# Expert weights split during the attention steps, routing in two halves, first steps reordered

## The reference

```
a   = (LN(x) Wq^T)(LN(x) Wk^T)^T * D^-0.5 + adj      12 heads of 32
x   = x + softmax(a) (LN(x) Wv^T + bv) Wo^T + bo      a row of zeros gives 0
u   = LN(x);  logits = mean over nodes(u) router_w^T + router_b
e0, e1 = the two greatest of 4 experts; gates = softmax of their logits
y   = sum over k of gate_k * (act_ek(u w1[ek] + b1) w2[ek] + b2) + u
out = x + LN(y) * ln_g + ln_b                         act: gelu, silu, mish, gelu
```

## Time and profile before

| | us |
|---|---|
| median of three runs | 1681.1 |
| the profiled execution, its own time | 1679.88 |
| its span in the profile | 1678.1 |
| PE busy | 1598.1 (95%) |
| DVE busy | 1191.3 (71%) |
| ACT busy | 953.4 (57%) |
| POOL busy | 826.9 (49%) |
| DMA moved | 159.32 MB, mean 95 GB/s |

### The profile page before, as it was taken

The page is one execution under the profiler, slowest core; times in us unless marked ns, Lnnn a source line. Parts: engine busy times, 40 slices in busy tenths (PEclk is TensorE's granted clock), DMA queues, the critical chain, the costliest instruction groups (busy, mean ns, idle before and its releaser), DMA issues.

```text
span 1678.1 us, 44889 instructions
## 1 busy us (share of the span) xinstructions
PE 1598.1 (95%) x12732; PEld 1531.1 (91%) x12733; DVE 1191.3 (71%) x3613; ACT 953.4 (57%) x2780; POOL 826.9 (49%) x1239
## 2 busy tenths in 40 slices
PE   6999999999999999837999999999999999999997
PEld 6899999999999999727999999999999999999997
DVE  4788888888888887776666665666776766567764
ACT  4888888888888888744332332332433423243332
POOL 2777777777777777760233333323333233323333
PEclk9999999999999999958999999999999999999999
DMA  7233333333333332550122222222222222221221
GB/s 242 67 116 114 120 121 121 116 116 121 121 121 121 121 119 97 178 216 20 62 72 70 70 70 70 70 70 70 70 70 70 70 70 70 70 70 62 79 64 36
DMA packets 81260, 159.32 MB, mean 95 GB/s; under 512 B 8672, under 2 KB 46560, under 8 KB 80992
## 3 DMA queue, kind: packets, MB, share of 16 engines
q1 hardware_dynamic: 81120, 157.58, 27.6%
HBM read 94.64 MB, written 62.91 MB: 94 GB/s over the span
## 4 chain that ended last, share of the span: by engine, by line
PE 88%; DVE 5%; ACT 2%; issue 2%; SPq 1%; POOL 1%; DMA 1%; DVEq 0%; POOLq 0%; ACTq 0%
PE bank L368 68%; PE bank L437 5%; PE bank L526 5%; PE bank L396 3%; PE bank L460 3%; PE bank L477 2%; PE bank L469 1%; PE bank L446 1%; DMA x_in<-in_x 1%; DVE half_t L1027 1%; DVE inverse L1034 1%; DVE inverse L1030 1%; ACT at_hi L688 1%; ACT inverse L721 1%; ACT prob L599 1%
## 5 line engine op out<-in xcount | busy, mean ns | idle before, releaser
L368 PE MATMUL bank<-w_hi,ut_in 128*128 x1536 | 423.2, 343 | 32.3 <-issue 27.9
L599 ACT ACTIVATE prob<-att,neg_max 128x128 f32<-128x128 f32 x768 | 297.4, 391 | 34.4 <-DVE neg_max L871 34.3
L368 PEld LDWEIGHTS bank<-w_hi,ut_in 128*128 128x128 f32 x1536 | 280.8, 189 | 37.0 <-issue 37.0
L987 DVE SCALAR_TENSOR_TENSOR at_lo<-bank,gate_col,at_hi 128x384 fp32r<-128x384 f32 x256 | 146.1, 613 | 185.2 <-ACT at_hi L688 185.2
L368 PE MATMUL bank<-w_hi,at_hi 128*128 x768 | 258.0, 336 | 5.6 <-DVE at_lo L987 5.6
L368 PE MATMUL bank<-w_lo,ut_in 128*128 x768 | 257.9, 336 | 0.0
L368 PE MATMUL bank<-w_hi,at_lo 128*128 x768 | 257.1, 335 | 0.0
L368 PE MATMUL bank<-w_lo,at_hi 128*128 x768 | 256.7, 334 | 0.0
L688 ACT ACTIVATE at_hi<-bank,gate_col 128x384 fp32r<-128x384 f32 x256 | 134.5, 576 | 202.9 <-PE bank L526 201.0
L845 POOL TENSOR_SCALAR rs_z<-mv_z 128x1 f32<-128x1 f32 x64 | 14.7, 229 | 473.8 <-DVE mv_z L1053 473.8
L712 ACT ACTIVATE hid<-hid 128x384 f32<-128x384 f32 x192 | 95.1, 527 | 268.9 <-DVE hid L999 268.9
(11 more groups left out here) (136 smaller groups left out, 3820.9 us busy)
## 6 DMA issues: line engine op xcount, KB each, us to landing
xu_scratch<-xu SPq DMA_DIRECT2D x64, 384.0 KB, 2.3
ut_scratch<-ut_out SPq DMA_DIRECT2D x64, 384.0 KB, 2.7
ut_in<-ut_scratch SPq DMA_DIRECT2D x64, 384.0 KB, 2.9
xz<-xu_scratch SPq DMA_DIRECT2D x64, 384.0 KB, 3.0
x_in<-in_x SPq DMA_DIRECT2D x32, 384.0 KB, 4.4
xu<-in_x SPq DMA_DIRECT2D x32, 384.0 KB, 3.5
out_dram<-xz SPq DMA_DIRECT2D x64, 192.0 KB, 1.9
w_lo<-in_L_ffn_w SPq DMA_DIRECT2D x8, 1152.0 KB, 9.8
```

Of the source, the lines that this page charges most:

```text
L368: last = nc.tensor.matmul(acc, lhs[c][a], rhs[c][b], start=start and n == 0, stop=stop and n == len(terms) - 1)
L599: nc.scalar.activation(prob[g][:, hh, :], att[g][:, head, :], ACT.Exp, bias=neg_max[g][:, head:head + 1], scale=-1.0, accum_out=row_sum[g] ...
L987: nc.vector.scalar_tensor_tensor(out=flat(at_lo[:, s * DC:(s + 1) * DC, :]), in0=at_ps[s][:, 0:HALF], scalar=gate_col[:, col, 1:2], in1=fl ...
```

## The change

Each expert weight is cut into six pieces of 128x384: `PIECES` = 24 pieces of w1 and 24 of w2. From step 5 to step 52 each attention step splits one piece (ACT rounds it, DVE subtracts). The rest of w1 stays where it is; its rounded part, and both parts of w2, go by DMA to scratch tensors in DRAM. ACT's queue loads them back between step 56 and step 66, each where the tiles of stage 1 that it overwrites are free. The raw w1 is loaded in steps 1 to 4, w2 piece by piece. The routing runs for graphs 0 to 31 in portions in steps 53 to 60, and for graphs 32 to 63 within the first two graphs of stage 2; its softmax of two is a tanh. At the start the projection weights are transposed one by one between the first steps of x. Tiles are placed anew in SBUF to fit. Below, those lines, the semaphores' names, helpers that only move, and the bodies of the routing functions are left out: `route_greatest` is a maximum and two tensor_tensors, `route_expert` three operations and for k = 1 the gap of the two logits, `route_rest` two, `route_factors` three, `route_gates` three, all as in lines 1084 to 1104 but on 32 graphs. Indentation is shortened.

```diff
+    ROUTED = B // 2
+    PIECES = E * FC
+    FIRST = 5
...
+def piece(h):
+    return h - FIRST if 0 <= h - FIRST < 2 * PIECES else None
+def piece_tiles(j):
+    if j < PIECES:
+        e, c, s = j // FC, j % FC // 2, j % 2
+        return w1_lo[:, e, c, s * HALF:(s + 1) * HALF], stage_hi[j % 3][:]
+    return stage_lo[j % 3][:], stage_hi[j % 3][:]
...
     load_x(0)
-    for m, w in enumerate((Wq, Wk, Wv, Wo)):
-        sp.dma_start(w_raw[m][:], w.rearrange("(c p) d -> p c d", p=P)).then_inc(w_loaded[m], 16)
+    load_projection(0)
+    load_projection(1)
     load_x(1)
-    sp.dma_start(bv_wide[:], bv.rearrange("(o d) -> o d", o=1).partition_broadcast(P)).then_inc(small_loaded, 16)
-    sp.dma_start(bo_wide[:], bo.rearrange("(o d) -> o d", o=1).partition_broadcast(P)).then_inc(small_loaded, 16)
+    load_projection(2)
+    sp.dma_start(bv_wide[:], bv.rearrange("(o d) -> o d", o=1).partition_broadcast(P)).then_inc(bv_loaded, 16)
+    load_projection(3)
     for t in range(2):
...
+    sp.dma_start(bo_wide[:], bo.rearrange("(o d) -> o d", o=1).partition_broadcast(P)).then_inc(small_loaded, 16)
...
-    for e in range(E):
-        sp.dma_start(w1_lo[:, e].bitcast(F32), w1[e].rearrange("(c p) f -> p c f", p=P)).then_inc(w1_loaded, 16)
...
+    def load_piece(j):
+        e, c = (j - PIECES) // FC, (j - PIECES) % FC
+        reached(sp, lo_stored[j % 3], 16 * ((j - PIECES) // 3))
+        sp.dma_start(stage_lo[j % 3][:].bitcast(F32), w2[e, c * P:(c + 1) * P, :]).then_inc(piece_loaded[j % 3], 16)
+    def store_piece(j):
+        sp.wait_ge(piece_lo, j + 1)
+        if j < PIECES:
+            e, c, s = j // FC, j % FC // 2, j % 2
+            sp.dma_start(w1h_dram[e, :, c, s * HALF:(s + 1) * HALF], stage_hi[j % 3][:].bitcast(F32)).then_inc(hi_stored[j % 3], 16)
+        else:
+            e, c = (j - PIECES) // FC, (j - PIECES) % FC
+            sp.dma_start(w2_dram[1, e, :, c], stage_hi[j % 3][:].bitcast(F32)).then_inc(hi_stored[j % 3], 16)
+            sp.dma_start(w2_dram[0, e, :, c], stage_lo[j % 3][:].bitcast(F32)).then_inc(lo_stored[j % 3], 16)
...
+        if piece(h - 1) is not None:
+            store_piece(piece(h - 1))
+        if piece(h + 1) is not None and piece(h + 1) >= PIECES:
+            load_piece(piece(h + 1))
+        if 1 <= h <= E:
+            load_w1(h - 1)
...
-    load_ut(0, 0)
-    sp.dma_start(b1_wide[:].rearrange("p e s f -> p (e s f)"), b1.rearrange("(o e) f -> o (e f)", o=1).partition_broadcast(P)).then_inc(wide_loaded, 16)
-    load_ut(1, 1)
-    sp.dma_start(b2_wide[:].rearrange("p e d -> p (e d)"), b2.rearrange("(o e) d -> o (e d)", o=1).partition_broadcast(P)).then_inc(wide_loaded, 16)
     load_xz(0, 0)
     load_xz(1, 1)
-    sp.dma_start(lng_wide[:], ln_g.rearrange("(o d) -> o d", o=1).partition_broadcast(P)).then_inc(wide_loaded, 16)
-    sp.dma_start(lnb_wide[:], ln_b.rearrange("(o d) -> o d", o=1).partition_broadcast(P)).then_inc(wide_loaded, 16)
-    load_xz(2, 2)
-    load_xz(3, 3)
+    sp.wait_ge(xbo_done, B)
+    sp.wait_ge(v_done, B)
+    load_ut(0, 0)
+    load_ut(1, 1)
...
+    def load_rest():
+        sp.wait_ge(routed, 2)
+        load_xz(2, 2)
+        load_xz(3, 3)
...
         finish(b, m)
+        if isinstance(b, int) and b == 0:
+            load_rest()
...
     def project_qk(h):
         m, t = h % 2, pair(h + 2)
+        if h < 0:
+            pe.wait_ge(wt_lo_done, (m + 1) * DC)
...
+    def logits(half):
+        graphs = slice(half * ROUTED, (half + 1) * ROUTED)
+        pe.wait_ge(pooled_done, (half + 1) * ROUTED)
...
+        reached(pe, routed, half)
+        for e in range(E):
...
+                last = nc.tensor.matmul(bank[7][:, D + e * ROUTED:D + (e + 1) * ROUTED], rw_wide[:, c, e, :], pooled[:, graphs, c],
...
+    pe.wait_ge(ident_ready, 2)
+    transpose_weights(0)
...
-        if h == -2:
+        if h == 0:
             pe.wait_ge(wt_lo_done, 4 * DC)
...
         if has(h + 2):
             project_v(h + 2)
+        if h == B - 11:
+            logits(0)
...
         if has(h + 5):
             transpose_x(h + 5)
+        if h == -4:
+            transpose_weights(1)
+            transpose_weights(2)
+        if h == -2:
+            transpose_weights(3)
...
     pe.wait_ge(routed, 1)
+    pe.wait_ge(w1h_loaded, 16 * E)
...
                 first_layer(b, k, m, lap, first_e)
+            if isinstance(b, int) and b == 0 and k == 1:
+                logits(1)
...
+                    pe.wait_ge(w2_loaded, 32 * E)
                 second_layer(b - 1, k, m - 1, second_e)
...
+    def round_piece(j):
+        raw_piece, rounded = piece_tiles(j)
+        if j < PIECES:
+            act.wait_ge(w1_loaded[j // FC], 16)
+        else:
+            act.wait_ge(piece_loaded[j % 3], 16 * ((j - PIECES) // 3 + 1))
+        reached(act, hi_stored[j % 3], 16 * (j // 3))
+        nc.scalar.activation(rounded, raw_piece.bitcast(F32), ACT.Copy).then_inc(piece_hi, 1)
+    def load_w1_hi(e):
+        act.dma_start(w1_hi[:, e].bitcast(F32), w1h_dram[e]).then_inc(w1h_loaded, 16)
+    def load_w2(half, e):
+        act.dma_start((w2_lo, w2_hi)[half][:, e].bitcast(F32), w2_dram[half, e]).then_inc(w2_loaded, 16)
...
+    def load_under_projections(h):
+        if h == FIRST + 2 * PIECES + 3:
+            for p in range(3):
+                act.wait_ge(hi_stored[p], 16 * (2 * PIECES // 3))
+                act.wait_ge(lo_stored[p], 16 * (PIECES // 3))
+            load_w1_hi(0)
+        if h == B - 4:
+            act.wait_ge(xn_done, B)
+            act.dma_start(b2_wide[:].rearrange("p e d -> p (e d)"), b2.rearrange("(o e) d -> o (e d)", o=1).partition_broadcast(P)).then_inc(wide_loaded, 16)
+            act.wait_ge(qk_mm, 2 * B - 2)
+            load_w1_hi(1)
+        if h == B - 3:
+            act.wait_ge(qk_mm, 2 * B)
+            load_w1_hi(2)
+    def load_under_values():
+        act.wait_ge(v_mm, B)
+        load_w1_hi(3)
+        act.dma_start(b1_wide[:].rearrange("p e s f -> p (e s f)"), b1.rearrange("(o e) f -> o (e f)", o=1).partition_broadcast(P)).then_inc(wide_loaded, 16)
...
+    def load_under_scores():
+        act.wait_ge(s_mm, B)
+        load_w2(0, 0)
+        act.wait_ge(exp_done, HEADS * (B - 1))
+        act.wait_ge(fold_done, FOLDS * (B - 1))
+        load_w2(0, 1)
+    def load_under_exps():
+        act.wait_ge(exp_done, HEADS * B)
+        act.wait_ge(fold_done, FOLDS * B)
+        load_w2(0, 2)
+    def load_under_probs():
+        act.wait_ge(pt_mm, PTC * B)
+        load_w2(0, 3)
+    def load_under_attended():
+        act.wait_ge(ot_done, B)
+        load_w2(1, 0)
+        load_w2(1, 1)
+    def load_under_output():
+        act.wait_ge(wo_mm, B)
+        load_w2(1, 2)
+        load_w2(1, 3)
...
+    def tanh_of_gap(half):
+        act.wait_ge(gap_done, half + 1)
+        nc.scalar.activation(g_tmp[:, 1, :], g_tmp[:, 0, :], ACT.Tanh, scale=0.5).then_inc(tanh_gap, 1)
...
     for h in STEPS:
+        if h == B - 2:
+            load_under_values()
+        if h == B + 1:
+            load_under_attended()
         if has(h - 2):
             round_o(h - 2)
+        if h == B:
+            nc.scalar.preload_act_table(ACT.Gelu)
         if has(h + 4):
             round_x(h + 4)
+        if h == -3:
+            round_weights(1)
+        if piece(h) is not None:
+            round_piece(piece(h))
+        if h == B - 4:
+            tanh_of_gap(0)
         if has(h):
             exps(h, (0, 1))
+        if h == B - 1:
+            load_under_scores()
         if has(h - 3):
             normalise_x1(h - 3)
+        if h == B + 2:
+            load_under_output()
         if has_qk(h):
             take_qk(h)
+            load_under_projections(h)
         if has(h - 1):
             take_probs(h - 1, 0)
             take_probs(h - 1, 1)
+        if h == B:
+            load_under_probs()
         if has(h - 3):
             round_u(h - 3)
         if has(h - 1):
             take_inverse(h - 1)
         if has(h + 5):
             normalise_x(h + 5)
+        if h == -5:
+            round_weights(0)
+        if h == -3:
+            round_weights(2)
+        if h == -2:
+            round_weights(3)
         if has(h):
             exps(h, (2, 3))
-    act.wait_ge(w1_loaded, 16 * E)
...
-    for m in range(2 * E):
...
-        nc.scalar.activation(hi, lo.bitcast(F32), ACT.Copy).then_inc(split_hi, 1)
...
-    nc.scalar.preload_act_table(ACT.Gelu)
+        if h == B - 1:
+            load_under_exps()
     act.wait_ge(routed, 1)
...
+            if isinstance(b, int) and (b, k) == (1, 1):
+                tanh_of_gap(1)
...
-    for m in GPSIMD_SPLITS:
-        hi, lo = expert_weights(m)
-        pool.wait_ge(split_hi, m + 1)
-        nc.gpsimd.tensor_tensor(lo, lo.bitcast(F32), hi.bitcast(F32), ALU.subtract).then_inc(gpsimd_lo, 1)
     pool.wait_ge(routed, 1)
-    pool.wait_ge(wide_loaded, 64)
...
+    def rest_of_piece(j):
+        raw_piece, rounded = piece_tiles(j)
+        dve.wait_ge(piece_hi, j + 1)
```

(99 more changed lines are left out.)

197 lines of the change are left out of this document (87 added, 110 removed).

## The result

The changed kernel takes 1676.7 us (median of 20 runs, 1673.1 to 1679.7) against 1681.4 us (20 runs, 1680.1 to 1684.1): ratio 0.9972, 95% interval 0.9965 to 0.9979. That is 4.8 us faster where 22.8 were forecast, and outside the range of 1650 to 1672. The profiled execution of the changed kernel took 1678.37 us (span 1676.6), 1.7 more than its median, that of the kernel before 1.6 less than its own: so the two traces lie 1.5 us apart where the medians lie 4.8 apart.

The account below looks back on a forecast made before the run. PE, busy 95% of the span, was taken as the bound, so only its waits count. Terms -6 + 0 + 2 + 0.5 + 3 - 24.3 + 2 = -22.8 from 1679.9 gave 1657.1, as a median 1658 us; range 1650 to 1672.

Parts of the forecast that it names:

- a gap of over 15 us: Between the stages: last ut_scratch store to first expert matmul, forecast about 8 us; over 15 would show the prediction wrong.
- The later stage is unchanged: Stage 2 after its first graphs: no change in time, no term in the sum.
- SP waits for the last store as before: Between the stages: ut_in issued at about 731.0 to 731.4, landing in 6 us; -24.3 us, from -27.4 to -17.8.
- rival A: Reload of w2 is late for the second layer, 14.2 MB through the queues: 1664 to 1671 us, chance 0.17.
- First graphs of stage 2: Second logits on PE and DVE's routing operations, partly within PE's existing waits: +2 us, from 0 to 6.
- End of attention: Last steps of stage 1: ACT issues 14 DMAs, about eight count at 0.4 us: +3 us, from 0 to 11.
- Start: Before the first projection only one weight's rest and three graphs of x; projection at 15 us: -6 us, -8 to -2.
- I count no new stall: At the start: x tiles of graphs 4 and 5 cause no new stall, as w1 loads move to steps 1 to 4.
- Pieces: Steps 5 to 52: ACT's copy and DVE's subtraction fit into their waits: 0 us, as a bound 14 in all.
- rivals B and C: B: steps grow 0.3 us, 1672 us, chance 0.12; C: the piece bounds DVE's and ACT's loop, 1687 us, chance 0.06.
- The risk that the earlier trace suggested: Attention steps: DVE's subtraction, reading two SBUF tiles, may wait 0.5 us for POOL's pow; 27 us at most.
- Routing of the first half: Steps 53 to 60: logits on PE's path +2 us, DVE's portions +0.5 (0 to 2).

Follow-up runs that it names:

- experiment 1: VectorE's stage-2 loop moved by unused instructions: changed kernel plus 186 increments 1670.4 us, or by an untaken branch 1667.0; kernel before plus 70 1692.0, plus 35 1681.7.
- experiment 2: Changed kernel with the four loads of w2's rounded part issued by SyncE between the stages, not by ScalarE in stage 1's last steps: 1664.1 us.
- experiment 5: Changed kernel with the second half of the routing moved from stage 2's first graphs into the gap between the stages: 1672.9 us.
- experiment 3: Changed kernel with the first two loads of w2's rest moved some 9 us later, together with the third: 1673.9 us.
- experiment 6: Changed kernel with the raw w1 loads at the start again: 1689.0 us; kernel before with only those loads moved to steps 1 to 4: 1681.9 us.

## Why the prediction was wrong

The direction was right and the size was not; the prediction's own sign of being wrong, a gap of over 15 us, came true with 18.4. By its steps, in the traces' own sum (-1.5 us against -22.8 forecast):

- **"The later stage is unchanged": the step that failed most, 9.4 us.** Its instructions are unchanged; the place of VectorE's loop in its code is not, and experiment 1 shows that this alone makes the loss, in either kernel. The prediction put this term at nothing, with no range: it counted added instructions by their duration only, never how far they push what stands behind them.
- **"SP waits for the last store as before": 7.5 us.** The gap was forecast at -24.3 with -17.8 as its worst and gave -16.8. The load behind the store took 5.45 us (6 taken), but the store itself 10.74, where the step had it at the 2.4 of before. The prediction added up 14.2 MB for rival A and looked for their harm at w2's first use; there was none, the harm was at the small transfer on the path (experiment 2).
- **First graphs of stage 2: +2 taken, 0 to 6 allowed, +6.9 measured.** The logits took 2.76 us (1.3 to 2.7 taken). The portions were held to fall into TensorE's waits; they stood ahead of `hid` and made these waits longer, and after the longest the clock was low (experiment 5).
- **End of attention: +3 taken, +7.1 measured, inside 0 to 11.** The issues cost what was said (0.33 to 0.53 each, 1.48 once). Missing was the residual's load among the transfers that w2 can hold up; experiment 3's trace puts some 2 us on it, in a wait that differs between executions. Another 2.1 are the low clock, of which 1.3 are chance and no term of the change.
- **Start: -6 taken, -8 to -2 allowed, -10.8 measured, a miss to the good side.** The first projection came at 12.9 us, 15 being forecast, and the scores 11.5 us after it where 12.4 had passed before. That "I count no new stall" from the x tiles was right, but the w1 loads were counted as no gain either; experiment 6 shows them to be a condition of the whole gain.
- **Pieces: 0, right, to 0.1 us over 48 steps,** so rivals B and C fell. The cover that was named held: ACT's 0.49 us ahead of the exponentials and DVE's 0.46 ahead of `ot` are filled. The risk that the earlier trace rows suggested came the other way round: VectorE's subtraction didn't wait for POOL's `pow`, the `pow` took 0.94 us and not 0.57, and POOL had the time, so that TensorE paid nothing.
- **Routing of the first half: +2.5, right (+2.7).**
- **Rival A,** the reload late at its use, did not occur: no wait of the second layer for w2, even in experiment 2, where half of it is loaded only from 733 us on.

The five misses add up to 21.3 us (9.4, 7.5, 4.9, 4.1 and 0.2, less 4.8 at the start), the whole difference between -22.8 and the -1.5 of the traces. Since several of them change from execution to execution, the medians' -4.8 is not told apart in this way.

## What to carry to other kernels

Code added ahead of a loop moves the loop: if an engine stands for nothing nameable at each turn and the instruction queue moves packets there, shift the loop's code before looking for another cause. When bulk loads are put beside a pipeline's tail, ask first which small transfers are on the path in that time (the last store, the last input), not when the bulk is wanted. And where two conditions hold back the same event, as the order of the start and the queue ahead of `x_in`, undoing one shows nothing.

## What the runs showed of the hardware

- At a turn of the loop VectorE stands 1.1 us when its code is still held, and 3.1 to 4.5 us when it isn't; 51 packets (0.42 MB) went through the instruction queue in 600 us. 35 more instructions ahead of the loop than in the kernel before cost nothing, 70 cost 9.9 us, and at 256 more nothing is lost over the loop again.
- Semaphore increments on VectorE follow each other by 93 ns: 80 of them ended at 8.5 us and the first scores came 5.8 us later than in the trace without them.
- Router logits in 24 matmul records took 5.38 us with 64 columns and 5.33 with 32, both at the low clock, and 2.76 with 32 at full clock: here their time went with the clock and not with the columns.
- A store of 0.39 MB took 2.3 us without, and 9.8 to 10.7 us in six traces with, 4.6 MB of another engine's loads issued ahead of it in a different queue.
- In the profiled executions the first scores of kernels with the same start came between 24.4 and 26.2 us, and POOL's wait for the residual was 0.5, 3.9, 4.4, 4.8, 5.7 and 7.7 us in six with the same loads ahead of it. After the same wait of 1.95 us the granted clock was 1.00 over the next nine matmuls in one execution and the low level in another. These differences may be behind the wider spread of the changed kernel's times (6.5 us between lowest and highest of 20, 4.0 before); no run tests it.
